# One core, a rotation and three attention blocks: the blocks' prologue inside the setup, scores of two heads as alternating row tiles, and 27 stack transfers

## The chip, the cores and the metric

The kernel runs on one core of one Trainium2 chip. The metric is the device time of one execution in microseconds. The kernel before takes 2118.55 us, the median of three runs.

## The reference

The input `x` has 16 samples of 256 tokens with 288 channels; `cond` has one row of 288 per sample. First, a rotation: a 64-dimensional basis is taken from `P` by a QR factorisation, and each sample gets a rotation of that subspace by the matrix exponential of a skew matrix. Then three attention blocks, alike in form:

```python
v = silu(cond) @ W.T + b                 # 2016 entries of a skew matrix A, per sample
Q, _ = qr(P);  z = x @ Q                 # z @ expm(A) replaces z inside x
x = x + (z @ expm(A) - z) @ Q.T
...
for each of three layers:
    sh_a, sc_a, g_a, sh_m, sc_m, g_m = split(silu(cond) @ W_ada + b_ada, 6)
    h = layer_norm(x) * (1 + sc_a) + sh_a
    q, k, v = heads(h @ W_qkv + b_qkv)   # 16 heads of 18
    x = x + g_a * (softmax(q @ k.T * scale) @ v @ W_proj + b_proj)
    h = layer_norm(x) * (1 + sc_m) + sh_m
    x = x + g_m * (gelu(h @ W_fc1 + b_fc1) @ W_fc2 + b_fc2)   # 288 -> 1152 -> 288
```

## The kernel before

**Two programs one after the other.** `rotation_setup` (L51) does the rotation and the modulation rows of all layers; `layers` (L914) does the blocks. The setup's QR is a Householder sweep in nine phases of up to eight columns on DVE. One column is a chain of small operations: size and sign of the pivot (L771, L772), pivot (L779), turned column (L793), reciprocal (L799), factor (L805), next column (L813), outer product (L819), and the update of the tile (L785); then ACT takes square roots (L374) for `norm_col` (L833). DVE's squarings of the exponential (L724) and PE's pieces (transposes of x L490, its projection L498) fill the gaps. After the QR come the modulation rows (L539, L543), the differences (L625, two samples as two row tiles of 64 rows on PE), the sums on DVE (L906) and 16 stores to the output tensor; SP waits for all of them before `layers` starts. There POOL stages `w_in`, DVE splits it, sample 0 is read back, and its layer norm taken.

**The half-step.** `layers` runs 48 half-steps, one per layer and sample. The work is a software pipeline: in half-step `it` the core does the shifted scores, exponentials and weighted values of sample `it`, the projection and MLP of `it - 1`, and the queries, keys, values and first scores of `it + 1`. Each engine runs its own list of this in an order written by hand; counting semaphores join them.

**Precision.** fp32 data is split in a high and a low part (fp32r). A product is three products, so the three pieces of 18 channels of a head are laid below each other in a stack. `q_stack` and `k_stack` hold eight units of two heads. In `k_stack` each unit has two columns of 256, one for each head, with zeros in the rows of the other head; the two heads of a unit share 108 rows (`PAIR_ROWS`). They are filled from the `qk` tiles by SP in `stacks` (L1199): group A (units 0 to 4) is 9 transfers, 3 of queries (L1189) and 6 of keys (L1195), which wait for the fifth shifted unit of the sample before; group B (units 5 to 7) is 15, and waits for the last shifted unit.

**Scores.** `score_unit` (L1706) is two matmuls of 108 rows and 512 columns into `scores` (L1718), two sets of banks taken in turn. DVE takes the maxima (`unit_max`, L1968) of 128 by 1024 numbers. Unit `u` waits for the maxima of unit `u - 2`, so one unit is always in hand:

```python
if u < 2: pe.wait_ge(s_exp, 8 * it - 1 + u + PRE_EXP)
else:     pe.wait_ge(s_max, 8 * it + u - 1)
```

After all eight, the maxima are transposed (L1728), negated (ACT L1491), and put as one more row each into `q_stack` by two transfers. `shifted_unit` (L1732) then computes scores minus maximum, transposed, in four matmuls of 110 rows and 256 columns (L1741), and ACT takes the exponentials (L1501). The weighted values (L1755, four column tiles of 32) give also the sums; these go by ACT's queue to a scratch tensor and back (L1515, L1520), DVE takes reciprocals (`inverse`, L1973), and four more transfers spread them (L1530) into `inv_sum`. ACT issues the four between the activations of the MLP's hidden tiles, the last after the last of these (L1544). `normalise` (L1980, two DVE operations) waits for them. In DVE's order it stands before the maxima of unit 3; the gating of the MLP's first token tile (`gate_down`, L2016) stands before those of unit 5:

```python
for u in range(8):
    if u == 3:
        normalise(it)
    if u == 5 and before:
        gate_down(it - 1, 0)
    if after:
        unit_max(it + 1, u)
```

PE's list around the scores (L1845 to L1876): `up` (L1780, five uses) makes the hidden tiles, unit 0 comes ahead of the last `up` and unit 1 behind it, then transposes (L1651), then six parts of `down` (L1635 with `w_down`, nine matmuls each, the bias of a tile of tokens L1789), with units 2 to 6 behind the parts 0 to 4 and unit 7 behind unit 6. POOL makes the low parts (L1294), among them those of the hidden tiles.

Of the kernel before, what the change touches and what calls it, by code (L numbers as in the profile page):

```python
# [6 lines left out]
F32 = mybir.dt.float32  # L7
# [8 lines left out]
L = 3  # L16
# [22 lines left out]
PAIR_ROWS, SHIFTED_ROWS = 6 * HD, 6 * HD + 2  # L39
# [11 lines left out]
def rotation_setup(nc, dram, keep):  # L51


# [6 lines left out]
    mods, g_rot, ident = keep["mods"], keep["g_rot"], keep["ident"]  # L60
    with ExitStack() as ctx:
# [3 lines left out]
        def sem(name):  # L65
            return ctx.enter_context(nc.semaphore(name))
# [13 lines left out]
        w_ada = sb("w_ada", [KC + 1, L, NCH, ADA])  # L80

        shared = sb("w_rot_x", [P, R * R * NCH])
        w_rot = [shared[0:KC + 1, n * 1024 * NCH:(n + 1) * 1024 * NCH].rearrange("k (c e) -> k c e", c=NCH) for n in range(4)]
        x_all = shared[:, 0:B * XF].rearrange("p (s t c) -> p s t c", s=B, t=2)
        v_rot = sb("v_rot", [P, 4, SKEW_COLS])
# [7 lines left out]
        ef = sb("ef", [P, NPAIR, 2, R])  # L93
# [19 lines left out]
        size = sb("size", [P, 2])  # L113
# [15 lines left out]
        z_all = sb("z_all", [P, NPAIR, T])  # L129
        f_c = sb("f_c", [P, NPAIR, R])  # L130
# [20 lines left out]
        s_eye = sem("s_eye")  # L151
        s_ready = sem("s_ready")
# [4 lines left out]
        s_v_st = sem("s_v_st")  # L157
        s_a_ld = sem("s_a_ld")
# [20 lines left out]
        s_size = sem("s_size")  # L179
        s_pivot = sem("s_pivot")  # L180
        s_recip = sem("s_recip")
        s_turn = sem("s_turn")
        s_factor = sem("s_factor")
        s_next = sem("s_next")
        s_outer = sem("s_outer")
        s_update = sem("s_update")
# [13 lines left out]
        s_inv_norm = sem("s_inv_norm")  # L200
# [14 lines left out]
        s_out_st = sem("s_out_st")  # L215
# [6 lines left out]
        SQUARES = {5: range(0, 6), 6: range(6, 15), 7: range(15, 24), 8: range(24, FILLS)}  # L222

        PAIRS = {2: (0,), 4: (1, 2), 5: (3,), 6: (4,), 7: (5,), 8: (6,), PHASES: (7,)}
        POWERS_AT, SERIES_AT = 3, 4
# [13 lines left out]

        @block.sync  # L240
        def _(sp):
            sp.dma_start(p_nat[:, :, :], dram["p_nat"]).then_inc(s_p, 16)
            sp.dma_start(unit[GRAM, GRAM_COLS], dram["ident"][0:R, 0:R]).then_inc(s_unit, 16)
            sp.dma_start(unit[TOP, TOP_COLS], dram["ident"][0:R, 0:R]).then_inc(s_unit, 16)
            sp.dma_start(low[GRAM, GRAM_COLS], dram["lower"][:, 1, :]).then_inc(s_low, 16)
# [11 lines left out]
            for n, (a, b) in enumerate(GROUPS):  # L257
                if n == 0:
                    sp.wait_ge(s_skew_ps, 1)
                if n == 1:  # L260
                    sp.wait_ge(s_skew_ps, 4)
                    sp.wait_ge(s_a_ld, 16 * 8)
# [1960 lines left out]
```

## Time and profile before

| | us |
|---|---|
| median of 3 runs (2117.92 to 2121.7) | 2118.55 |
| the profiled execution | 2125.66 |
| its span | 2123.9 |
| PE busy | 1966.4 (93%) |
| DVE / ACT / POOL busy | 1224.8 / 1107.5 / 1015.8 |
| PE matmuls of scores L1718 / L1741, busy | 241.9 / 246.5 |
| maxima L1968, busy | 460.7 |
| starts of the first and of the last maxima transposes (L1728) | 233.56 and 2055.18 |

The span is cut in a setup, from 0 to about 176 us, a filling of the pipeline, and 48 half-steps. Between the first and the last pair of maxima transposes lie 47 intervals; most of the ordinary ones are 37.69 us long, and some with the weights of a new layer are longer. PE's busy time counts the overlap of matmuls once. A row of the timeline gives start, length, engine, line, what is written from what, partitions by elements, and the number of instructions. A matmul's length includes the pipeline; how far starts lie apart tells more of what it costs.

### The profile page before, as it was taken

The numbers are of one execution on the slowest core, as the hardware profiler recorded it, in microseconds if no ns is written. First come the engines' busy times: TensorE is split into PE (matmuls) and PEld (weight loads), VectorE is DVE, ScalarE is ACT, GpSimd is POOL, SyncE is SP. The second block draws the span as 40 slices with busy tenths as digits, with TensorE's granted clock in tenths as the row PEclk, the third lists the DMA queues.
The fourth block names the chain that finished last, engine by engine and source line by source line (L and its number), as shares of the span: only waits on it lengthen the run. The fifth ranks groups of instructions, "written<-read, shape, count | busy, mean of one in ns | idle before, by whom it ended". The sixth has DMA issues, their size and how long they took to land. (4 is left out here: it accounts for less than half of the span.)

```text
span 2123.9 us, 50051 instructions
## 1 busy us (share of the span) xinstructions
PE 1966.4 (93%) x16599; PEld 1746.1 (82%) x16599; DVE 1224.8 (58%) x2813; ACT 1107.5 (52%) x1906; POOL 1015.8 (48%) x1045
## 2 busy tenths in 40 slices
PE   4684599999999999999999999999999999999997
PEld 2553378998989988879989999888789899998986
DVE  7766375565655665574655556575656565565641
ACT  2222346656465564556465564654664655646552
POOL 2002164555545554655545545455645455454544
PEclk9887689999999999999999999999999999999998
DMA  6604243333233333343233333333432333333320
GB/s 167 160 13 142 83 135 107 95 89 99 80 108 91 93 95 95 111 131 100 80 104 88 98 99 84 99 88 93 144 96 81 103 88 99 99 83 100 86 80 25
DMA packets 138669, 207.65 MB, mean 98 GB/s; under 512 B 35204, under 2 KB 95778, under 8 KB 137518
## 3 DMA queue, kind: packets, MB, share of 16 engines
q1 hardware_dynamic: 111742, 171.06, 28.9%
q10 hardware_dynamic: 24192, 27.94, 4.7%
q0 software_dynamic: 2640, 7.44, 1.2%
q8 instruction: 53, 0.87, 0.2%
q14 instruction: 42, 0.34, 0.1%
HBM read 99.81 MB, written 20.82 MB: 57 GB/s over the span
## 5 line engine op out<-in xcount | busy, mean ns | idle before, releaser
L1968 DVE TENSOR_REDUCE maxima<-scores 128x4 f32<-128x1024 f32 x384 | 460.7, 1222 | 185.7 <-PE scores L1718 180.9
L1294 POOL TENSOR_TENSOR hidden<-g_full,hidden 128x512 fp32r<-128x512 f32 (+1 forms) x240 | 280.5, 1177 | 356.8 <-ACT hidden L1544 355.8
L1501 ACT ACTIVATE probs<-scores 128x1024 f32<-128x1024 f32 x384 | 383.2, 1026 | 95.2 <-PE pv_ps L1755 57.1
L1780 PE MATMUL mlp_ps<-h_mlp,w_up 128*128 128x256 f32 (+1 forms) x3024 | 405.6, 287 | 8.2 <-ACT hidden L1544 4.7
L1780 PEld LDWEIGHTS mlp_ps<-h_mlp,w_up 128*128 128x128 f32 (+1 forms) x3024 | 377.5, 191 | 42.0 <-issue 19.3
L1635 PE MATMUL mlp_ps<-w_down,hidden 128*128 128x288 f32 x2592 | 388.1, 294 | 0.0
L1635 PEld LDWEIGHTS mlp_ps<-w_down,hidden 128*128 128x128 f32 x2592 | 368.9, 188 | 18.5
L1718 PE MATMUL scores<-k_stack,q_stack 108*128 108x512 f32 x768 | 241.9, 407 | 22.4 <-DMA k_stack<-qk 18.4
L1741 PE MATMUL scores<-q_stack,k_stack 110*128 110x256 f32 x1536 | 246.5, 293 | 3.3 <-ACT probs L1501 2.0
L1741 PEld LDWEIGHTS scores<-q_stack,k_stack 110*128 110x128 f32 x1536 | 207.8, 191 | 32.1 <-issue 18.9
L1491 ACT ACTIVATE neg_max<-att_ps 16x256 fp32r<-16x256 f32 x48 | 18.0, 375 | 387.7 <-PE att_ps L1728 387.7
L1378 POOL TENSOR_TENSOR o_full<-o_full,inv_sum 128x512 f32<-128x512 f32 x96 | 140.5, 1484 | 156.6 <-DVE o_att L1980 156.6
L1973 DVE RECIPROCAL inv_few<-sums 128x32 f32<-128x32 f32 x48 | 16.9, 353 | 319.9 <-DMA sums<-sum_scratch 319.9
L1543 ACT ACTIVATE g_full<-mlp_ps 128x512 f32<-128x512 f32 (+1 forms) x240 | 133.7, 557 | 129.5 <-PE mlp_ps L1780 61.4
L1294 POOL TENSOR_TENSOR h_mlp<-h_full,h_mlp 128x512 fp32r<-128x512 f32 x48 | 72.6, 1511 | 259.0 <-DVE h_mlp L1934 258.8
L1755 PE MATMUL pv_ps<-probs,v_sb 128*32 128x256 f32 x3072 | 189.4, 388 | 0.6 <-ACT probs L1501 0.6
L1635 PE MATMUL mlp_ps<-w_out,o_att 128*128 128x288 f32 x1152 | 174.2, 302 | 4.0 <-issue 2.9
L1635 PEld LDWEIGHTS mlp_ps<-w_out,o_att 128*128 128x128 f32 x1152 | 159.9, 191 | 6.1 <-issue 3.5
L1718 PEld LDWEIGHTS scores<-k_stack,q_stack 108*128 108x128 f32 x768 | 128.0, 194 | 35.4 <-DMA k_stack<-qk 20.3
L1692 PE MATMUL att_ps<-h_att,w_in 128*126 128x256 f32 (+3 forms) x1008 | 137.6, 284 | 11.8 <-POOL h_att L1294 10.2
L1755 PEld LDWEIGHTS pv_ps<-probs,v_sb 128*32 128x32 f32 x3072 | 91.0, 111 | 65.5 <-issue 4.5
L1692 PEld LDWEIGHTS att_ps<-h_att,w_in 128*126 128x126 f32 (+3 forms) x1008 | 128.1, 185 | 12.9 <-issue 11.7
(221 smaller groups left out, 2865.9 us busy)
## 6 DMA issues: line engine op xcount, KB each, us to landing
q_stack<-qk SPq DMA_DIRECT2D x144, 180.0 KB
k_stack<-qk SPq DMA_DIRECT2D x288, 90.0 KB
inv_sum<-inv_scratch ACTq DMA_DIRECT2D x192, 128.0 KB, 2.7
k_stack<-qk SPq DMA_DIRECT2D x288, 54.0 KB
x_in<-out_x SPq DMA_DIRECT2D x48, 288.0 KB, 3.8
x_mid<-out_x SPq DMA_DIRECT2D x48, 288.0 KB, 4.2
out_x<-x_out SPq DMA_DIRECT2D x48, 288.0 KB, 3.1
q_stack<-qk SPq DMA_DIRECT2D x144, 72.0 KB
```

What stands on the lines that cost most here:

```text
L1294: tt(out, full, high.bitcast(F32), ALU.subtract).then_inc(signal, 1)
L1378: tt(o_full[:, half, :], o_full[:, half, :], inv_sum[:, half, :], ALU.mult).then_inc(s_o_norm, 1)
L1491: evict(neg_max[:, :], att_ps[0:H, 0:T], ACT.Copy, scale=-1.0).then_inc(s_neg, 1)
L1501: evict(probs[:, u % 4, :, :, :], scores[u % 2][:, :, :, :], ACT.Exp, scale=SCALE)\
L1543: evict(g_full[:, n % 2, 0:width], bank[:, 0:width], ACT.Gelu_apprx_tanh).then_inc(s_gelu, 1)
L1635: last = mm(out, a(left), c(weights[w]), start=start and n == 0, stop=stop and n == total - 1)
L1692: last = mm(qk_bank[n][0:cols.stop - cols.start, (m % 2) * T:(m % 2 + 1) * T], w[:, cols], h, start=count == 0, stop=count == 6)
L1718: last = mm(scores[u % 2][:, qt, :, :], q_stack[r, u, qt * P:(qt + 1) * P], k_stack[r, u, :, :], start=True, stop=True)
L1741: last = mm(scores[u % 2][:, par, kt, :], k_stack[r, u, par, kt * P:(kt + 1) * P], q_stack[r, u, :], start=True, stop=True)
L1755: last = mm(pv_ps[32 * i:32 * i + 32, (g % 2) * T:(g % 2 + 1) * T], v_sb[:, kt, 4 * g + i, :], probs[:, u % 4, i % 2, kt, :], start=kt == ...
L1780: last = mm(up_bank[n % 2][:, (m % 2) * T:(m % 2 + 1) * T], w[:, m * P:(m + 1) * P], h, start=count == 0, stop=count == 6)
L1968: nc.vector.tensor_reduce(out=maxima[:, :, :, u], in_=scores[u % 2][:, :, :, :], axis=AX.X, op=ALU.max).then_inc(s_max, 1)
```

## The change

**The prologue in the setup.** `rotation_setup` returns at once. A new function `prepare`, called inside `layers` when only the first tiles are laid out, does the setup. In it POOL also stages the three pieces of `w_in`, ACT makes their high parts in the phases 6 to 8 of the QR and DVE the low parts behind it; ACT fills the constants of `k_stack` and `v_sb`; the rotated sample 0 stays in `x_in`, and its statistics and `x_hat` are made among the sums of the other samples. The wait for the 16 output stores has moved into `layers`. In the QR step the size operation is gone (the pivot is now one operation with the sign), waits are merged, the update stands ahead of the reciprocal and the spreading ahead of `column_norms`. Small loads went to ACT's queue, the `w_rot` loads stand second on SP's, the skew rows go in halves by SP and POOL, powers and series one phase earlier, pair 7 and the modulation rows of layer 0 into the last phase, and only one layer's rows stand among the differences, where two stood.

**Row tiles.** `k_stack` has one set of columns per unit and no zeros. A head's rows start at 0 or at 64, and its 54 rows (55 with the maximum) are multiplied alone, as a row tile. Two heads alternate, and two units are done in one visit, which waits for both units before:

```diff
-            def score_unit(it, u):
+            def score_units(it, u):
 
                 if u == 0:
                     pe.wait_ge(s_stack_a, PIECES_A * (it + 1) + 16)
-                if u == 5:
+                    pe.wait_ge(s_exp, 8 * it + PRE_EXP)
+                else:
+                    pe.wait_ge(s_max, 8 * it + u)
+                if u == 4:
                     pe.wait_ge(s_stack_b, PIECES_B * (it + 1) + 16)
-                if u < 2:
-                    pe.wait_ge(s_exp, 8 * it - 1 + u + PRE_EXP)
-                else:
-                    pe.wait_ge(s_max, 8 * it + u - 1)
-                r = slice(0, PAIR_ROWS)
-                for qt in range(2):
-                    last = mm(scores[u % 2][:, qt, :, :], q_stack[r, u, qt * P:(qt + 1) * P],
-                              k_stack[r, u, :, :], start=True, stop=True)
-                last.then_inc(s_score, 1)
+                    pe.wait_ge(s_stack_k, PIECES_K * (it + 1))
+                for v in (u, u + 1):
+                    for qt in range(2):
+                        for par in range(2):
+                            r = slice(R * par, R * par + HEAD_ROWS)
+                            last = mm(scores[v % 2][:, par, qt, :], q_stack[r, v, qt * P:(qt + 1) * P],
+                                      k_stack[r, v, :], start=True, stop=True, tile_position=(R * par, 0))
+                    last.then_inc(s_score, 1)
...
+            def shifted_units(it, u):
 
                 if u == 0:
                     pe.wait_ge(s_neg_st, 32 * it + 32 + 16)
-                if u >= 2:
-                    pe.wait_ge(s_exp, 8 * it + u - 1 + PRE_EXP)
+                else:
+                    pe.wait_ge(s_exp, 8 * it + u + PRE_EXP)
...
                 for n in range(6):
+                    if after and n % 2 == 0:
+                        score_units(it + 1, n + 2)
                     if before:
                         down(m, n // 3, n % 3)
-                    if after and n < 5:
-                        score_unit(it + 1, n + 2)
-                    if after and n == 4:
-                        score_unit(it + 1, 7)
```

`score_units(it + 1, 0)` stands ahead of the fourth `up` (n of 3). ACT's list now has the exponentials of units 0 and 1 between the first and the second query and key eviction. DVE's list in the half-step is as it was.

**The transfers.** Each of 27 moves 18 rows. Group A is 12 by SP, group B 9 queries by SP, and the 6 keys of units 5 to 7 go by POOL, in `last_keys`, behind the same condition as group B:

```diff
                 for j in range(3):
-                    into_stack(j, Q_PARTS[j], slice(0, 5), slice(0, PAIR), slice(0, 5), s_stack_a)
-                for j in range(3):
                     for par in range(2):
-                        head_into_stack(j, par, K_PARTS[j], slice(0, 5), PAIR + HD * par, slice(0, 5), s_stack_a)
+                        head_into_stack(sp, q_stack, j, par, Q_PARTS[j], slice(0, 5), HD * par, slice(0, 5), s_stack_a)
+                        head_into_stack(sp, k_stack, j, par, K_PARTS[j], slice(0, 5), PAIR + HD * par, slice(0, 5), s_stack_a)
...
+            def last_keys(it, first=False):
...
+                if not first:
+                    pool.wait_ge(s_st, 8 * it + PRE)
...
+                        head_into_stack(pool, k_stack, j, par, K_PARTS[j], slice(2, 5), 2 * PAIR + HD * par, slice(5, 8), s_stack_k)
```

**How the instructions move.** First PE's list, from the third to the seventh unit of scores (`scores<-k_stack,q_stack`) among the parts of `down` (`mlp_ps<-w_down,hidden`). Before:

```order
L1718 MATMUL scores<-k_stack,q_stack 128x512 x2
L1635 MATMUL mlp_ps<-w_down,hidden 128x288 x9
L1718 MATMUL scores<-k_stack,q_stack 128x512 x2
L1791 REGISTER_ALU
L1635 MATMUL mlp_ps<-w_down,hidden 128x288 x9
L1715 REGISTER_ALU
L1718 MATMUL scores<-k_stack,q_stack 128x512 x2
L1789 MATMUL mlp_ps<-b_down,ones_l 128x288
L1635 MATMUL mlp_ps<-w_down,hidden 128x288 x9
```

The same place of the change, the third and fourth unit, the fifth and sixth:

```order
L1824 MATMUL scores<-k_stack,q_stack 128x256 x8
L1895 ISA
L1896 MATMUL mlp_ps<-b_down,ones_l 128x288
L1898 REGISTER_ALU
L1739 MATMUL mlp_ps<-w_down,hidden 128x288 x18
L1816 REGISTER_ALU
L1818 ISA
L1819 REGISTER_ALU
L1824 MATMUL scores<-k_stack,q_stack 128x256 x8
```

Where one unit stood behind nine matmuls, two now stand ahead of eighteen.

SP's list, the transfers of one sample into the stacks, before:

```order
L1189 DMA q_stack<-qk 36x1280 x3
L1195 DMA k_stack<-qk 18x5x256 x6
L1189 DMA q_stack<-qk 36x512
L1195 DMA q_stack<-qk 18x256 x2
L1189 DMA q_stack<-qk 36x512
L1195 DMA q_stack<-qk 18x256 x2
L1189 DMA q_stack<-qk 36x512
L1195 DMA q_stack<-qk 18x256 x2
L1195 DMA k_stack<-qk 18x3x256 x6
```

The end of group A and the beginning of group B in the change (ten transfers like the first two stand ahead):

```order
L1282 DMA q_stack<-qk 18x1280
L1282 DMA k_stack<-qk 18x1280
L1282 DMA q_stack<-qk 18x768
L1282 DMA q_stack<-qk 18x512
L1282 DMA q_stack<-qk 18x256
```

Group A has grown from 9 to 12 transfers, group B on SP shrunk from 15 to 9.

## Rows read from the trace of the kernel before

**Rows 1.** One half-step: busy time (instructions) of each engine, granted clock, DMA share, GB/s.
```profile
1000.00:1037.70 37.70, 37.70 (x320) 34.40 (x319) 21.53 (x40) 21.83 (x36) 19.75 (x20) 1.00 0.35 94
```

**Rows 2.** The page's costliest groups: busy time, mean ns, idle before and releaser.
```profile
L1718 PE MATMUL scores<-k_stack,q_stack 108*128 108x512 f32 x768 | 241.9, 407 | 22.4 <-DMA k_stack<-qk 18.4
```

**Rows 3.** PE's timeline in that half-step, first scores and `down`.
```profile
1045.08 0.38 PE L1789 MATMUL mlp_ps<-b_down,ones_l 128*128 128x288 f32 x1
...
1046.49 0.63 PE L1718 MATMUL scores<-k_stack,q_stack 108*128 108x512 f32 x2
1046.95 1.36 PE L1635 MATMUL mlp_ps<-w_down,hidden 128*128 128x288 f32 x9
1048.15 0.63 PE L1718 MATMUL scores<-k_stack,q_stack 108*128 108x512 f32 x2
```

**Rows 4.** PE's timeline in the setup, row tiles of 64 rows, two samples.
```profile
168.09 0.51 PE L625 MATMUL chain_a<-g_rot,z_all 64*128 64x288 f32 x1
...
168.10 0.51 PE L625 MATMUL ps_a<-g_rot,z_all 64*128 64x288 f32 x1
...
168.43 0.40 PE L625 MATMUL chain_a<-g_rot,z_all 64*128 64x288 f32 x1
...
168.68 0.40 PE L625 MATMUL chain_b<-g_rot,z_all 64*128 64x288 f32 x1
```

**Rows 5.** PE's timeline, weighted values and the `up` behind them.
```profile
1034.69 1.94 PE L1755 MATMUL pv_ps<-probs,v_sb 128*32 128x256 f32 x32
1036.56 1.88 PE L1780 MATMUL mlp_ps<-h_mlp,w_up 128*128 128x256 f32 x14
```

**Rows 6.** PE's timeline at two narrow stretches: starts two groups of four apart.
```profile
1035.58 0.61 PE L1755 MATMUL pv_ps<-probs,v_sb 128*32 128x256 f32 x8
...
1036.02 0.61 PE L1755 MATMUL pv_ps<-probs,v_sb 128*32 128x256 f32 x8
```

**Rows 7.** DVE's timeline around the maxima of one half-step.
```profile
1047.15 1.23 DVE L1968 TENSOR_REDUCE maxima<-scores 128x4 f32<-128x1024 f32 x1 [1.22 <-PE scores L1718]
1048.29 1.28 DVE L1980 TENSOR_TENSOR o_att<-o_full,inv_sum 128x512 fp32r<-128x512 f32 x2
1049.49 2.35 DVE L1968 TENSOR_REDUCE maxima<-scores 128x4 f32<-128x1024 f32 x2
1051.76 0.45 DVE L2016 TENSOR_TENSOR gated<-mlp_ps,gate_f 128x288 f32<-128x288 f32 x1
```

**Rows 8.** Issues on SP's queue (SPq, group A) and on ACT's (ACTq).
```profile
1028.81 2.58 SPq L1189 DMA_DIRECT2D q_stack<-qk  x3
1031.43 5.85 SPq L1195 DMA_DIRECT2D k_stack<-qk  x6
...
1044.59 0.59 ACTq L1530 DMA_DIRECT2D inv_sum<-inv_scratch  x1
```

**Rows 9.** Part 6 of the page: issues, KB each, us from issue to landing.
```profile
inv_sum<-inv_scratch ACTq DMA_DIRECT2D x192, 128.0 KB, 2.7
```

**Rows 10.** POOL's timeline in the filling of the pipeline: issues of transfers.
```profile
177.72 1.69 POOL L1303 DMA_DIRECT2D staging<-in_w_in  x3 [0.83 <-POOL minus_half L1277]
```

**Rows 11.** Waits before 180 us: who waited for whom, total, times, longest.
```profile
DVE norm_col L833 <- ACT gram_norm L374: 11.0, 5, 5.2
```

**Rows 12.** PE's timeline from the end of the QR to the first queries and keys.
```profile
136.48 0.86 PE L490 MATMUL xt_ps<-ident,w_rot_x 128*96 128x128 f32 x6
...
141.05 1.37 PE L539 MATMUL ada_ps<-w_ada,silu_c 96*16 96x352 f32 x8
...
153.66 0.79 PE L539 MATMUL ada_ps<-w_ada,silu_c 96*16 96x352 f32 x8
...
156.30 0.70 PE L438 MATMUL xt_ps<-u_t,f_c 64*64 64x288 f32 x4
...
187.66 1.09 PE L1651 MATMUL att_ps<-ident,x_hat 128*128 128x128 f32 x4 [14.73 <-DVE x_hat L1921]
...
199.32 3.25 PE L1692 MATMUL att_ps<-h_att,w_in 128*126 128x256 f32 x14 [10.15 <-POOL h_att L1294]
```

More of the change, by code:

```diff
@@ new lines, in layers @@
+        b_down = sb("b_down", [P, C], F32R)
+        ones = sb("ones_l", [P, P], F32R)
+        warm = sb("warm", [P, 1])
+        x_mid = sb("x_mid", [P, 2, C])
+        x_one = sb("x_one", [P, 2, C])
+        x_out = sb("x_out", [P, 2, C])
+        gated = sb("gated", [P, 2, C])
+        gate_a = sb("gate_a", [P, C])
+        gate_f = sb("gate_f", [P, C])
+        h_full = sb("h_full", [P, 3, T])
+        h_att = [sb(f"h_att{i}", [P, 3 - i, T], F32R) for i in range(2)]
+        h_mlp = [sb(f"h_mlp{i}", [P, 3 - i, T], F32R) for i in range(2)]
@@ new lines, in layers @@
+        qk = [sb(f"qk{i}", [QK_ROWS, QK_TILES, T], F32R) for i in range(2)]
+        q_stack = sb("q_stack", [P, H // 2, T], F32R)
+        maxima = sb("maxima", [P, 2, 2, H // 2])
+        neg_max = sb("neg_max", [H, T], F32R)
+        probs = sb("probs", [P, 4, 2, 2, T])
+        o_full = sb("o_full", [P, 2, 512])
+        sums = sb("sums", [P, 32])
+        inv_few = sb("inv_few", [P, 32])
+        inv_sum = sb("inv_sum", [P, 2, 512])
+        o_att = [sb(f"o_att{i}", [P, 2, 512], F32R) for i in range(2)]
@@ new lines, in in_place @@
+        def in_place(name, shape):
+            with nc.sbuf_tensor(f"{name}_raw", shape, F32) as raw:
+                pass
+            return raw, sb(f"{name}1", shape, F32R)
+        w_up = [sb("w_up0", [P, 3, FF], F32R)]
+        up_raw, up_low = in_place("w_up", [P, 2, FF])
+        w_up.append(up_low)
+        w_down = [sb("w_down0", [P, NF, C], F32R)]
+        down_raw, down_low = in_place("w_down", [P, NF, C])
+        w_down.append(down_low)
+        hidden = [sb(f"hidden{i}", [P, NF, T], F32R) for i in range(2)]
@@ L1165, in at, with head_into_stack @@
             return isinstance(b, int) and b == n
+        Q_PARTS, K_PARTS = (0, 1, 0), (0, 0, 1)
+        def head_into_stack(engine, stack, j, par, part, src, row, units, signal):
+            first = R * par + HD * j
+            engine.dma_start(stack[first:first + HD, units, :].bitcast(F32),
+                             qk[part][row:row + HD, src, :].bitcast(F32)).then_inc(signal, 16)
         @block.sync
```

609 lines of the change are left out of this document (313 added, 296 removed).

## The prediction

> **What bounds the kernel now.** I read the view of stretches first, then PE's timeline of one half-step, then the waits, and last DVE's timeline and the queues around the two places where PE's list changes. In a half-step PE has no gap at the full granted clock, while DVE, ACT and POOL are busy for 21.53, 21.83 and 19.75 of 37.70 us [rows 1]. So 48 half-steps are bound by PE, and what another engine gains is worth nothing there unless PE waits for it. Ahead of them it is otherwise: PE stood still for 14.73 and 10.15 us before it had its first queries and keys at 199.32 [rows 12], and the score matmuls waited 18.4 us for keys in their stack, all in the first samples [rows 2]. The change touches both parts. It shortens the first, once. In the second it alters PE's work and the order of the waits, 46 to 47 times, so that 0.1 us per half-step weighs as much as 4.7 us of setup.
>
> **PE's work per half-step.** A unit of scores costs 0.46 us before (from 1046.49 to the next start at 1046.95) [rows 3], a shifted unit about the same, so two units 0.94. In the change two units are eight matmuls of 256 columns, in four pairs. The nearest rows for two row tiles are those of the setup: the two start 0.01 apart, so they run at once, and pairs follow each other by 0.25, only after the first by 0.34 [rows 4]. Those are fp32; the split data streams 512 columns in 0.23 [rows 3], so a pair of 256 columns costs 0.12 and four 0.48. What is left is the price of the change between whole rows and tiles. Leaving tiles is seen behind the weighted values: eight groups take 8 x 0.22 = 1.74 [rows 6], but the next `up` starts 1.87 after the first [rows 5], 0.13 more, and entering shows 0.34 - 0.25 = 0.09 [rows 4]. The matmul behind the first also looked late in narrower stretches, so I take 0.2 for a change, 0.4 for a visit. Then a visit costs 0.88, against 0.94: a gain of 0.06, in eight visits 0.5 us per half-step. The ends: 0.48 for a visit if a change of tiles costs nothing, 1.36 if two row tiles did not run at once.
>
> The Trainium skill speaks of both. "TensorE: Matmul & The Clock Gate", "Measured speedup vs the span model", gives the span of packed matmuls as the duration of one plus about 4 ns for each further tile, with no term for a change; by that a visit would cost about 0.5. "TensorEngine Tiling (Array Packing)", "Key Properties", says that a change of the tiling mode drains TensorE, without a price. The rows with 0.13 and 0.09 more [rows 4 to 6] side with the second.
>
> **The waits that pairs bring.** Before, a unit waited for the unit two ahead of it; one unit was always in hand while DVE read the other. Now both banks must be read before a visit begins, and DVE's list is unchanged, so what stands in it between two maxima comes on the path.
>
> *Units 4 and 5* wait for the maxima of unit 3, ahead of which the normalisation stands. From the start of the visit for 2 and 3: 0.66 until the first maxima start (1046.49 to 1047.15) [rows 3, 7], 1.14 for them, 1.20 for the normalisation (1048.29 to 1049.49), 1.22 for the second and 0.05 for the signal: 4.27. PE meanwhile has the visit, 0.88, and two parts of `down` with the bias, 1.41 + 1.20 = 2.6 [rows 3]: 3.5. It stands for 0.8. More, if the sums' reciprocals come late: the last of the four transfers that spread them is issued behind the last hidden tile at 1044.59 [rows 8] and lands 2.7 later [rows 9], at 1047.3, 1.0 ahead of its reader now. In the change this tile is finished about 0.4 later, since a whole visit stands ahead of the fourth `up`, while the visit for 2 and 3 comes ahead of `down` and so 1.4 earlier. The normalisation then starts some 0.8 late and the stand is 1.6. I take 1.4.
>
> *Units 6 and 7* wait for the maxima of unit 5, ahead of which stands the gating of the first token tile, which needs the third part of `down`. From the visit for 4 and 5: 0.88 + 1.20 for the part, some 0.3 until DVE reads it, 0.45 for the gating, 1.22 for the maxima: 4.05, against 0.88 + 1.20 + 1.41 = 3.5 on PE. 0.55.
>
> *Group A.* Nine transfers are issued in 8.5 us (1028.81 to 1037.28) [rows 8], keys 0.98 and queries 0.86 each. The new ones are contiguous on both sides, as the queries were, and half as tall; I take 0.82, an estimate, and twelve give 9.8. The ends: 0.75, or 0.98 as the keys now, 9.0 and 11.8. Their release, the fifth shifted unit, comes with the sixth now, behind the first weighted values; they land some 2 us behind the last issue. Their reader, the visit for 0 and 1, has moved 1.7 us ahead, from the fifth `up` to the fourth. By this account it waits 0.2 to 0.5; I take 0.35, and 1.7 for the upper end.
>
> *Shifted units.* ACT needs 1.0 per unit and has PE's other work beside it; only pairs wait for pairs. 0.2.
>
> The sum: -0.5 + 1.4 + 0.55 + 0.35 + 0.2 = **+2.0**; part of a stand is slack for the next (a late visit for 0 and 1 makes the normalisation less late), so I take **+1.9**. In 46 half-steps: +87.
>
> *POOL's six* cost 6 x 0.56 = 3.4 us of POOL [rows 10]. They stand between the low part of the MLP's input and the first hidden tile, where POOL has nothing to do; it is busy for 19.75 of 37.70 [rows 1]. Nothing, if they land before the visit for 4 and 5, some 8 us later. Without this cover the hidden tiles, and `down` with them, would come up to 3.4 late.
>
> **The setup, once.** The QR: the waits for ACT's roots, 11.0 in five phases [rows 11], shrink since the spreading and ACT's roots no longer stand in front of each other, and PE's first loads come earlier: -8, between 0 and -15. One operation of a step less of nine, but the pivot is a longer one on the chain behind the sign: 0, between -7 and +5. Pair 7 out of the stretch behind the QR: 136.48 to 141.05, -4.6 [rows 12]. One layer's modulation rows fewer in the differences: 153.66 to 156.30 [rows 12], -3 with the columns. From there to the first queries and keys at 199.32: PE's stand for the normalised sample 0 is gone but for some 4 us, -10.9; POOL's low part need not wait for staging, -5.1; the wait for the last stores, -2. Together **-34**. First group A +1.2, the first scores with a shorter group B -3.4, and the stack waits of the first two half-steps, 7 of the 18.4 [rows 2], -7. All once: **-43**, between -25 and -58.
>
> **The sum.** The profiled execution took 2125.66 (span 2123.9). 2125.7 - 43 + 87 = 2169.7. The median of the runs is 7.1 below the profiled one, so it becomes **2162**.
>
> **Rivals.** *(a) Changing tiles costs next to nothing*: a visit 0.5 to 0.55, -3.2 per half-step. The stands grow, since DVE's chain does not shrink: 1.75 for units 4 and 5, 0.6, 0.65 for group A, 0.6 for the shifted pairs: +3.6. That is +0.4, 19 in all, and with the setup 2095: faster. For it: rows 4 show only 0.09 for entering. Against it: 0.13 for leaving, and the unchanged list of DVE. It decides from +0.8 per half-step downwards, where the setup's gain still pays. Cheaper waits at the price I forecast (the slack absorbs most) end in the same place; both together 0.22. (The skill's span rule is this case.) *(b) Row tiles are serial here*: a visit 1.36, +3.8 after shorter stands, 2118 - 43 + 175 = 2250. Against it stand the two starts 0.01 apart [rows 4], though of fp32 and 288 columns; 0.06. *(c) Transfers are late*: group A at 0.98 each and POOL's six not landed before units 4 and 5: another +1.1, 2212; 0.12. *(d) The setup gains little*, -15, with the loss as forecast: 2190; 0.06. *(e) The merged waits cost nothing and changes do, so nothing moves*: 0.04.
>
> **How the numbers follow.** My forecast, 2162 with 2130 to 2190 around it, has 0.5. What the measurement can tell from no change is 0.2%, 4.2 us. Faster by more: (a), 0.24 with the fringe of (e). Within: 0.05. Slower: the rest, 0.71. The range takes in (a)'s point, 2095, with 7 below it, and (c) up to 2212; outside stay (b) and the far side of (a). 2088 to 2212.
>
> **What would show it.** Right: intervals of the maxima transposes near 39.6; gaps on PE of about 1.4 and 0.6 us before the visits for 4 and 6, released by DVE's maxima, and DVE idle before the normalisation for a spread transfer; the two heads' matmuls 0.01 apart with a visit of 0.9; first queries and keys near 165. Wrong: visits of 0.5 to 0.6, or maxima that are always ahead (the loss is then too large); or gaps before the visit for 0 released by a stack transfer of over 1 us; or a granted clock below 1.00 in the half-steps, which I count as none because the gaps are short.

## The result and the profile after

The changed kernel takes 2316.37 us (median of 4 runs, 2307.9 to 2326.05), the kernel before 2119.69 beside it. The ratio is 1.093 (95% interval 1.088 to 1.098): slower by 197 us. The forecast was 2162, slower by 43. The direction was right and the size was not, and the range (to 2212) does not hold it.

The profiled execution has a span of 2312.1 us against 2123.9, 188.2 more. The starts of the maxima transposes cut it in three. The first pair comes at 209.53 instead of 233.56 (the setup gained 24.0); from there to the last pair, at 2237.18, lie 2027.6 us instead of 1821.6 (206.0 more in 47 intervals, 4.4 each); the rest is 74.9 instead of 68.7 (6.2 more).

Part 1 of the page of the changed kernel; it answers to the row of before in the table ahead, PE 1966.4 (93%):

```profile
PE 1980.1 (86%) x17367; PEld 1690.4 (73%) x17367; DVE 1210.3 (52%) x2735; ACT 1111.2 (48%) x1930; POOL 1156.3 (50%) x1319
```

PE is busy for more time and a smaller share. Two half-steps of the changed kernel that follow each other, in the view of stretches (columns as in [rows 1]):

```profile
1037.50:1078.40 40.90, 36.92 (x336) 31.95 (x335) 21.57 (x40) 21.78 (x36) 22.86 (x26) 1.00 0.31 87
1078.40:1121.40 43.00, 39.96 (x337) 35.03 (x335) 21.57 (x40) 21.77 (x36) 22.85 (x26) 0.92 0.30 82
```

The first runs at the full clock. PE's work has fallen from 37.70 to 36.92, and 4.0 us of standing have come. The second is 2.1 us longer: PE's busy time has 3.0 more for the same matmuls, its standing 0.9 less, and the granted clock is 0.92. So there are two losses, gaps and a slower clock.

PE's timeline of the changed kernel in one half-step, first scores (L1824) and `down`:

```profile
1017.99 0.74 PE L1824 MATMUL scores<-k_stack,q_stack 54*128 54x256 f32 x8 [1.60 <-DMA k_stack<-qk]
1018.67 2.77 PE L1887 MATMUL mlp_ps<-h_mlp,w_up 128*128 128x256 f32 x21
...
1022.02 0.73 PE L1824 MATMUL scores<-k_stack,q_stack 54*128 54x256 f32 x8
1022.69 0.40 PE L1896 MATMUL mlp_ps<-b_down,ones_l 128*128 128x288 f32 x1
1022.93 2.54 PE L1739 MATMUL mlp_ps<-w_down,hidden 128*128 128x288 f32 x18
1028.83 0.74 PE L1824 MATMUL scores<-k_stack,q_stack 54*128 54x256 f32 x8 [3.36 <-DVE maxima L2072]
1029.50 1.45 PE L1739 MATMUL mlp_ps<-w_down,hidden 128*128 128x288 f32 x9
1030.79 0.29 PE L1896 MATMUL mlp_ps<-b_down,ones_l 128*128 128x288 f32 x1
...
1032.70 0.50 PE L1824 MATMUL scores<-k_stack,q_stack 54*128 54x256 f32 x4 [0.43 <-DVE maxima L2072]
```

A visit of two units takes 0.67 (1028.83 to 1029.50), and the nine matmuls behind it 1.29 where they took 1.20 [rows 3]: 0.76 in all, not 0.88. Row tiles and their changes are cheaper than forecast. Three of the four visits wait: 1.60 for the keys' stack, 3.36 for DVE, 0.43 for DVE. DVE at the same time:

```profile
1018.51 0.35 DVE L2077 RECIPROCAL inv_few<-sums 128x32 f32<-128x32 f32 x1 [8.49 <-DMA sums<-sum_scratch]
...
1022.57 1.23 DVE L2072 TENSOR_REDUCE maxima<-scores 128x4 f32<-128x1024 f32 x1 [1.50 <-PE scores L1824]
1026.17 1.29 DVE L2084 TENSOR_TENSOR o_att<-o_full,inv_sum 128x512 fp32r<-128x512 f32 x2 [2.37 <-DMA inv_sum<-inv_scratch]
1027.38 1.22 DVE L2072 TENSOR_REDUCE maxima<-scores 128x4 f32<-128x1024 f32 x1
```

DVE itself stands 2.37 us ahead of the normalisation, for the transfers that spread the reciprocals. These are late from their start. ACT's queue issues the store of the sums (`sum_scratch`), and the load behind it as soon as the store has landed. Before:

```profile
1037.33 0.53 ACTq L1515 DMA_DIRECT2D sum_scratch<-o_full  x1
1039.36 0.35 ACTq L1520 DMA_DIRECT2D sums<-sum_scratch  x1
```

and in the change:

```profile
1012.52 0.54 ACTq L1619 DMA_DIRECT2D sum_scratch<-o_full  x1
1016.21 0.36 ACTq L1624 DMA_DIRECT2D sums<-sum_scratch  x1
```

From issue to issue 2.03 us before, 3.69 now, for the same 16 KB. The load's issue stands ahead of the second hidden tile in ACT's list, so ACT stands too. The waits from 300 to 2000 us, changed kernel (total, times, longest):

```profile
PE scores L1824 <- DVE maxima L2072: 101.5, 67, 6.3
...
ACT g_full L1647 <- DMA sum_scratch<-o_full: 63.2, 23, 4.6
PE scores L1824 <- DMA k_stack<-qk: 57.9, 37, 2.5
```

101.5 + 57.9 = 159.4 us of PE's standing in some 40 half-steps, 4.0 each: 1.5 ahead of units 0 and 1, 2.3 ahead of 4 and 5, 0.3 ahead of 6 and 7. In the old kernel the score matmuls waited 0.6 us in that stretch. The clock fits: in the second of the two half-steps in the view of stretches two stretches of 5 us read

```profile
1095.00:1100.00 5.00, 4.65 (x39) 4.35 (x35) 0.00 (x0) 1.99 (x4) 1.51 (x2) 1.00 0.56 154
1100.00:1105.00 5.00, 3.88 (x25) 3.75 (x26) 2.56 (x3) 2.68 (x6) 2.56 (x2) 0.74 0.25 60
```

with a gap of 1.47 us that ended at 1101.12; behind it 21 `up` matmuls took 4.28 us where they take 2.77 at 1018.67. The clock was at its lower level (1.2 GHz) for a part of it. In the first of the two, gaps of 1.3 and 2.2 us left it at 1.00, so a lower clock follows a gap at times and not always. Over the whole trace the granted clock is below 1.00 in 32 of the 47 intervals of the change, and in 7 of those of the kernel before.

### The profile page after: what moved, and what is told of

It reads as the page before. It is cut to its first block and busy times, and to the rows that moved or that the text cites. A ratio compares the mean times of both kernels' runs of the same rounds, so it can differ in the third digit from the quotient of the medians.

```text
span 2312.1 us, 51564 instructions
## 1 busy us (share of the span) xinstructions
PE 1980.1 (86%) x17367; PEld 1690.4 (73%) x17367; DVE 1210.3 (52%) x2735; ACT 1111.2 (48%) x1930; POOL 1156.3 (50%) x1319
## 5 line engine op out<-in xcount | busy, mean ns | idle before, releaser
L1887 PE MATMUL mlp_ps<-h_mlp,w_up 128*128 128x256 f32 (+1 forms) x3024 | 437.0, 300 | 4.7 <-POOL h_mlp L1395 3.5
L1887 PEld LDWEIGHTS mlp_ps<-h_mlp,w_up 128*128 128x128 f32 (+1 forms) x3024 | 397.2, 202 | 40.5 <-issue 20.5
L1739 PE MATMUL mlp_ps<-w_down,hidden 128*128 128x288 f32 x2592 | 410.9, 313 | 0.0
L1824 PE MATMUL scores<-k_stack,q_stack 54*128 54x256 f32 x1536 | 150.8, 317 | 218.0 <-DVE maxima L2072 135.2
L1824 PEld LDWEIGHTS scores<-k_stack,q_stack 54*128 54x128 f32 x1536 | 109.9, 197 | 259.3 <-issue 196.7
L1862 PE MATMUL pv_ps<-probs,v_sb 128*32 128x256 f32 x3072 | 200.5, 391 | 0.8 <-ACT probs L1605 0.8
L1282 POOL DMA_DIRECT2D k_stack<-qk x288 | 152.7, 538 | 31.4 <-PE scores L1848 21.9
L1848 PE MATMUL scores<-q_stack,k_stack 55*128 55x256 f32 x1536 | 146.1, 310 | 4.4 <-ACT probs L1605 3.1
L1796 PE MATMUL att_ps<-h_att,w_in 128*108 128x256 f32 (+3 forms) x1008 | 137.5, 284 | 6.0 <-POOL h_att L1395 5.3
L1848 PEld LDWEIGHTS scores<-q_stack,k_stack 55*128 55x128 f32 x1536 | 106.4, 190 | 49.2 <-ACT probs L1605 29.7
L1862 PEld LDWEIGHTS pv_ps<-probs,v_sb 128*32 128x32 f32 x3072 | 86.0, 111 | 66.8 <-issue 12.9
```

Of the source, the lines that this page charges most:

```text
L1282: engine.dma_start(stack[first:first + HD, units, :].bitcast(F32), qk[part][row:row + HD, src, :].bitcast(F32)).then_inc(signal, 16)
L1739: last = mm(out, a(left), c(weights[w]), start=start and n == 0, stop=stop and n == total - 1)
L1796: last = mm(qk_bank[n][0:cols.stop - cols.start, (m % 2) * T:(m % 2 + 1) * T], w[:, cols], h, start=count == 0, stop=count == 6)
L1824: last = mm(scores[v % 2][:, par, qt, :], q_stack[r, v, qt * P:(qt + 1) * P], k_stack[r, v, :], start=True, stop=True, tile_position=(R * ...
L1848: last = mm(scores[v % 2][:, par, kt, :], k_stack[r, v, kt * P:(kt + 1) * P], q_stack[r, v, :], start=True, stop=True, tile_position=(R * ...
L1862: last = mm(pv_ps[32 * i:32 * i + 32, (g % 2) * T:(g % 2 + 1) * T], v_sb[:, kt, 4 * g + i, :], probs[:, u % 4, i % 2, kt, :], start=kt == ...
```

## The experiments

Fifteen versions were run; "load at" is the time from the issue of the sums' store to that of their load, "interval" the distance of the maxima transposes, both medians over half-steps of the profiled execution. Times are medians of all executions; the profiled one was 9 us or more above its median in three versions (2212 for the normalisation with a late load, 2137 for the four edits, 2174 for POOL in two parts), so their intervals read a little long.

| version | us | interval | load at |
|---|---|---|---|
| before | 2119.7 to 2123.3 | 37.70 | 2.04 |
| the change | 2316.4 | 42.33 | 3.96 |
| scores one unit at a time | 2240.7 | 41.32 | 3.99 |
| normalisation before unit 4 | 2189.7 | 39.20 | 3.96 |
| first visit later | 2299.2 | 41.47 | 4.05 |
| before, with pairs | 2280.0 | 41.10 | 2.04 |
| six keys on SP | 2291.0 | 42.03 | 2.37 |
| normalisation, late load | 2187.3 | 40.53 | 4.01 |
| the same, group A split | 2174.2 | 39.10 | 3.77 |
| single, late load | 2201.5 | 39.77 | 4.00 |
| four edits (POOL later) | 2128.1 | 37.90 | 2.39 |
| the same, all on SP | 2267.2 | 41.60 | 2.38 |
| single units, all on SP | 2123.3 | 38.27 | 2.38 |
| before, POOL's six | 2286.2 | 41.67 | 4.79 |
| POOL later alone | 2291.9 | 41.83 | 2.40 |
| POOL in two parts | 2160.5 | 38.82 | 2.39 |
| three and three | 2179.9 | 40.44 | 2.41 |

**Scores one unit at a time**, at the old places and with the old waits:

```diff
-                else:
-                    pe.wait_ge(s_max, 8 * it + u)
...
+                if u < 2:
+                    pe.wait_ge(s_exp, 8 * it - 1 + u + PRE_EXP)
+                else:
+                    pe.wait_ge(s_max, 8 * it + u - 1)
...
-                for v in (u, u + 1):
+                for v in (u,):
```

> The change, but the unit scores are made one unit at a time, at the places and with the waits of the kernel before (a unit waits for the unit two ahead); row tiles, transfers, setup and the pairs of shifted units stay. Theory W (the merged waits of the pairs of units make the loss, and the slower clock follows from PE's gaps): a unit costs 0.45, as before, the gaps before the third and fourth visit (2.4 and 0.3 us per half-step) go, the clock comes back to 1.00 in the ordinary half-steps, the interval of the maxima transposes falls from 42.3 to about 37.5 and the time to 2080 to 2100. Theory T (late transfers make it: 12 in group A and POOL's six): the wait for the keys' stack before unit 0 and the late sums stay, interval 40 to 41, time 2220 to 2260.

2240.7 lies in the range of theory T, and the load of the sums is at 3.99, as it says; the wait for keys ahead of unit 0 did not stay, since unit 0 comes one `up` later. The waits of PE for DVE's maxima went, as theory W said (101.5 us to under 4), but another of 71.7 us took their place.

```profile
ACT g_full L1647 <- DMA sum_scratch<-o_full: 72.8, 27, 3.3
PE mlp_ps L1888 <- ACT hidden L1648: 71.7, 39, 2.5
```

The store of the sums lands late, ACT stands for it, its second hidden tile is late, and so is PE's fourth `up`. So the merged waits are one cause and late transfers another, and in the change the stands ahead of the visits covered part of the second.

**The normalisation ahead of unit 4:**

```diff
-                    if u == 3:
+                    if u == 4:
                         normalise(it)
```

> The change with one line of DVE's list moved: the normalisation stands ahead of the maxima of unit 4 instead of unit 3. Theory W: the visit for units 4 and 5 no longer waits for the normalisation, nor for the transfers that spread the reciprocals; its gap of 2.4 us per half-step goes, that of the visit for 6 and 7 grows from 0.3 to about 1.3; the interval falls by 1.5 to 2.5, clock included, and the time by 70 to 120, to 2200 to 2245. If the clock is a cause of its own, or the transfers set the end, it falls by less than 30.

2189.7, 127 below the change, a little more than expected for one moved line: the largest part of the loss that a single edit gives back. The gap ahead of units 4 and 5 went; ahead of 6 and 7 it is 0.6 per half-step, and ahead of 0 and 1 still 1.6.

**The first visit one `up` later:**

```diff
-                        if after and n == 3:
+                        if after and n == UP_USES - 1:
                             score_units(it + 1, 0)
```

> The change with the visit for units 0 and 1 one use of up later, ahead of the last one, where unit 0 stood before. It now waits 1.5 us for the keys' stack. Theory T: that wait goes and the interval falls by 1 to 1.5 us, the time by 50 to 80. Theory W: PE then stands in the fourth up instead, since ACT's second hidden tile is late (it stands behind the wait for the sums' store), or the later maxima lengthen the gap before units 4 and 5; the time falls by less than 30 or rises.

2299.2, 17 less. The wait for keys went from the visit, and PE stood in the fourth `up` instead, 71.4 us for ACT's hidden tile from 300 to 2000: theory W's case, with the late store as its cause.

**The kernel before with pairs of units**, stacks, matmuls and transfers as they were:

> The kernel before with one part of the change: scores two units at a visit, with its merged waits and its places in PE's list. Stacks, transfers, matmuls of 108 rows and setup stay. Theory W: the visits for 4 and 6 wait for DVE as in the change; gaps of 0.8 to 2 and 0.3 to 0.6 us per half-step, interval 39 to 40.5, time 2180 to 2250. Theory T: with the old transfers nothing is late, interval below 38.2 and time below 2145.

2280.0, above the range that was expected. Its waits from 300 to 2000 us:

```profile
PE scores L1718 <- DVE maxima L1964: 63.4, 56, 3.0
...
PE scores L1718 <- DMA k_stack<-qk: 49.3, 22, 3.1
```

With the old transfers too, and that I had not thought of: the visit for 4 and 5 needs group B, one unit earlier than the unit 5 alone did, and SP's 15 issues come too late for it. Merged visits at the places of the change cost 157 us on the old kernel by themselves (2123.3 beside it).

**The six keys issued by SP**, behind its nine, and none by POOL:

> The change, but the six transfers of keys of units 5 to 7 are issued by SP behind its nine, and POOL issues none. In the change the store of the sums lands 1.9 us later than before (the load behind it is issued 3.96 instead of 2.04 after the store). Theory P (POOL's six crowd the DMA engines at that time): the load is issued at 2.0 to 2.7 again, the reciprocals' spread lands 1.5 us earlier, the interval falls by 1 to 1.5 us, the time to 2240 to 2275. Theory A (the twelve of group A do it, on SP's queue): the load stays at 3.5 to 4, the time within 20 of the change's 2316, or more if the last six land too late for units 4 and 5.

The load of the sums at 2.37: theory P, though the time is above its range. The gap ahead of the first visit went as well, and so POOL's six had delayed group A, not its own twelve issues. But SP issues the six behind its other 21, some 8 us after the load of the sums; so this run moves them in time as well as to another queue. But the six now come too late for units 4 and 5, and the sum is a gain of 25 only:

```profile
PE scores L1823 <- DMA k_stack<-qk: 97.1, 33, 3.3
```

**Normalisation and a late load of the sums** in ACT's list:

```diff
-                load_sums(it)
                 if before:
                     gelu(it - 1, 1)
+                load_sums(it)
```

> The change with the normalisation ahead of the maxima of unit 4, and in ACT's list the load of the sums behind the second hidden tile instead of ahead of it, so that ACT does not stand for the store with the tile behind it. Against the version with the first of these edits (2190): if the late second tile adds to the gap before the visit for 0 and 1, the time falls by 20 to 60; if only the keys' stack makes this gap (1.6 per half-step, released by a transfer of keys), it is 2180 to 2200.

2187.3 against 2189.7: the second case. Ahead of the first visit only the keys count.

**Group A split** between SP and POOL, keys of units 5 to 7 behind SP's nine, on top of the version before it:

> The version before it, and POOL issues the six transfers of keys of group A instead of those of units 5 to 7, which go behind SP's nine of group B. Group A is then issued in about half the time. Theory T2 (12 issues of 0.74 in a row make units 0 and 1 late): the gap of 1.6 us goes, the interval falls from about 38.8 to 36.5 to 37.5, and the time to 2060 to 2130, below the kernel before. If it is the landing under load rather than the issue, the gap stays above 1.0 and the time above 2140.

2174.2: the gap ahead of the first visit went (0.1 per half-step), as the first case has it, and the time stayed above 2140, as the second has it. The load is at 3.77: POOL's transfers of group A delay the sums as those of units 5 to 7 did. The waits for DVE grew (ahead of units 6 and 7 to 1.0, of 2 and 3 to 0.35), and PE stands 0.5 ahead of `down` for ACT's last hidden tile.

**Single units and a late load:**

> Scores one unit at a time at the old places, as in the first experiment (2241, with one gap of 1.7 us per half-step in the fourth up, released by ACT's hidden tile), and ACT's load of the sums behind the second hidden tile. If ACT standing for the store of the sums makes that gap: it goes, the interval is 37.0 to 38.0 and the time 2070 to 2120. If the tile is late for another reason: above 2200.

2201.5, inside the band that was to speak against it by a hair. The wait in the fourth `up` did go; 54.2 us in front of `down` for ACT's last hidden tile came in its place. Moving ACT's wait moved the stand.

**Four edits** (normalisation ahead of 4, gating ahead of 6, POOL's six behind its first hidden tile, small loads on SP first):

```diff
                     for n in range(UP_USES):
                         hidden_low(it - 1, n)
+                        if n == 0 and after:
+                            last_keys(it + 1)
```

> The change with four edits: the normalisation ahead of the maxima of unit 4, the gating of the first token tile ahead of those of unit 6, POOL's six transfers behind its first hidden tile instead of ahead of it, and the four small loads of the QR's start on SP's queue ahead of the w_rot loads. If POOL's six are what delays the store of the sums and group A: the load of the sums is issued 2.0 to 2.6 after the store (3.96 in the change), the gap before the visit for 0 and 1 falls from 1.6 to below 0.5, that for 6 and 7 to below 0.3; interval 36.5 to 38, time 2060 to 2120. The QR starts its first step at about 7.5 instead of 11.95 and the first maxima transposes come 4 to 5 earlier, 201 to 205. If it is group A on SP's queue: the gap of 1.6 stays, time above 2150.

2128.1 (ratio to before 1.003, interval 1.0015 to 1.005): 188 of the 197 us are back, though the time is 8 us above the expected range. Load at 2.39, the clock at 1.00 in 37 of 47 intervals (40 in the kernel before). What is left:

```profile
1029.78 3.12 POOL L1282 DMA_DIRECT2D k_stack<-qk  x6
1032.92 4.51 POOL L1395 TENSOR_TENSOR hidden<-g_full,hidden 128x512 fp32r<-128x512 f32 x4
...
1034.30 0.60 ACT L1649 ACTIVATE g_full<-mlp_ps 128x512 f32<-128x512 f32 x1 [2.42 <-POOL hidden L1395]
...
1036.25 0.40 PE L1898 MATMUL mlp_ps<-b_down,ones_l 128*128 128x288 f32 x1 [1.00 <-ACT hidden L1650]
```

POOL's six issues take 3.12 us, its next low part waits behind them, ACT's fourth tile for that, and PE 1.00.

**The same with all transfers on SP:**

> As the one before, but with the six issued by SP behind its nine (as in the experiment that gave 2291), POOL issues none. The load of the sums at 2.4, no gap before units 0 and 1. What is left is whether the last key lands before the visit for 4 and 5: 27 issues of 0.74 are 20 us behind the release. If it does, the interval is 36.5 to 38 and the time 2050 to 2120; if not, a gap of 1 to 3 us before that visit released by a transfer of keys, and 2140 to 2200.

2267.2, above what its bad case allowed: PE waits for keys, 112.8 us from 300 to 2000. For pairs the 27 issues of one queue, 0.74 us each, are a bound of their own.

**Single units, all on SP**, the old waits, no POOL:

> Scores one unit at a time at the old places with the old waits, shifted units in pairs, all 27 transfers on SP's queue, DVE's and ACT's lists as in the change, small loads on SP first. Theory: nothing is left that stands before PE but the pairs of shifted units, and those gain 0.27 per visit pair. Interval 36.5 to 37.5, clock 1.00 but for the special half-steps, time 2040 to 2095, faster than the kernel before. If even then the sums are late or the second hidden tile is: above 2120.

2123.3, the same as before (1.0007, 0.9994 to 1.0019), not faster. No waits of weight are left (0.8 per half-step in all, 0.6 before). What eats the gain is the change of tiles, which a single unit pays as often as a pair:

```profile
1034.40 0.50 PE L1824 MATMUL scores<-k_stack,q_stack 54*128 54x256 f32 x4
1034.83 1.46 PE L1738 MATMUL mlp_ps<-w_down,hidden 128*128 128x288 f32 x9
1036.22 0.50 PE L1824 MATMUL scores<-k_stack,q_stack 54*128 54x256 f32 x4
```

0.43 for the unit and 1.39 for the nine behind it, 1.82 where it was 0.46 + 1.20 = 1.66 [rows 3]. Eight times 0.16 are 1.3 us; the pairs of shifted units give back 4 x (0.94 - 0.76) = 0.7; the interval is 0.6 longer.

**The kernel before with POOL's six alone:**

> The kernel before with one part of the change: the six transfers of keys of units 5 to 7 are issued by POOL, at the place of the change; all else as it was. If POOL's six crowd out the others whatever the layout: the load of the sums is issued 3 to 4 instead of 2.04 after the store, ACT's second hidden tile and with it the fourth up come late, a gap of 0.5 to 2 per half-step, time 2145 to 2220. If it needs the twelve of group A beside them: within 10 of 2120.

2286.2, 165 more than before, for six transfers of 54 KB moved to another queue, and with that to another time: SP issued them from 7 us behind the store of the sums, POOL from 3.5 us ahead of it. It is well above the expectation, and the clearest run of the study:

```profile
1017.05 0.53 ACTq L1534 DMA_DIRECT2D sum_scratch<-o_full  x1
...
1021.19 0.35 ACTq L1539 DMA_DIRECT2D sums<-sum_scratch  x1
1021.72 0.60 ACT L1562 ACTIVATE g_full<-mlp_ps 128x512 f32<-128x512 f32 x1 [2.79 <-DMA sum_scratch<-o_full]
```

```profile
1022.85 2.74 PE L1800 MATMUL mlp_ps<-h_mlp,w_up 128*128 128x256 f32 x14 [1.97 <-ACT hidden L1563]
```

```profile
1013.54 3.73 POOL L1412 DMA_DIRECT2D k_stack<-qk  x6 [0.60 <-issue]
```

POOL issues from 1013.54 to 1017.3; the store issued at 1017.05 lands by 1021.2, in 4.1 us instead of 2.0; ACT stands 2.79, PE 1.97, and the fourteen matmuls behind that gap take 2.55 us to the next start where fourteen took 1.72 before the gap (from 1016.28), at a lower clock. ACT's stand for the store is 133.5 us from 300 to 2000, PE's for ACT's hidden tile 99.6.

**POOL's six later, nothing else:**

> The change with one edit: POOL's six transfers stand behind its first hidden tile instead of ahead of it; normalisation, gating and small loads as in the change. Theory P (their place crowds out group A and the sums): the load of the sums is issued 2.4 after the store, the gap before units 0 and 1 (1.5 per half-step) goes, that before units 4 and 5 shrinks but stays, since the normalisation still stands ahead of unit 3's maxima: interval 39 to 41, time 2170 to 2260. If the two causes were one and the same, the time would be near the 2128 of the version with all four edits.

2291.9, 24 less. Load at 2.40 and first visit in time (0.1 per half-step), as theory P has it, but above the range. The wait for DVE ahead of units 4 and 5 did not shrink, 2.4 per half-step for 2.3, and a new gap of 1.1 stands ahead of `down`, since POOL's low parts now wait behind its six issues:

```profile
PE scores L1826 <- DVE maxima L2074: 110.3, 65, 6.8
...
PE mlp_ps L1898 <- ACT hidden L1650: 43.9, 39, 2.6
```

The normalisation is hardly earlier. The load of the sums gained 1.6 us, but the last part of the spread lands 12.1 us after the store of the sums instead of 12.9: the six stand beside the store of the reciprocals now, which lands 2.6 us after its issue instead of 1.6. The edits add up to more than their parts: 127 for the normalisation alone, 24 for POOL alone, 188 for all four. How much of the rest the gating and the small loads give was not measured by itself.

**POOL's six in two parts**, three behind the first and three behind the third hidden tile:

> The version with four edits (2128), and POOL's six in two parts, three behind its first and three behind its third hidden tile. There the six in a row kept POOL for 3.1 us, ACT's fourth hidden tile waited 2.4 for POOL's low part, and PE stood 1.0 per half-step ahead of down. In threes: this gap falls below 0.3 and the time to 2075 to 2105, faster than the kernel before by 15 to 45. If another wait takes its place (the last three keys landing behind the visit for 4 and 5, or POOL's fourth low part late for down): 2110 to 2150.

2160.5, worse by 32. The gap ahead of `down` did fall (1.0 to 0.3 per half-step), but its second three stand beside the spread of the reciprocals: from the issue of its last part to its landing it takes 4.3 us instead of 2.7, and units 4 to 7 wait.

**Three by POOL, three by SP:**

> The version with four edits (2128), but POOL issues only the three transfers of the keys of the even heads of units 5 to 7 behind its first hidden tile, and SP the other three among its nine, 24 in all. If POOL being held by six issues makes the last gap (1.0 per half-step ahead of down), three issues halve it and nothing falls on the reciprocals' spread: gap below 0.3, time 2075 to 2110. If SP's 24 issues of 0.74 bring the last keys too late (17.8 us behind the release, 2 to 3 to land) a gap of 0.5 to 1 before units 4 and 5 takes its place: 2110 to 2140.

2179.9, above its bad case. PE's timeline:

```profile
1047.10 0.40 PE L1898 MATMUL mlp_ps<-b_down,ones_l 128*128 128x288 f32 x1 [0.48 <-ACT hidden L1650]
...
1051.52 0.73 PE L1826 MATMUL scores<-k_stack,q_stack 54*128 54x256 f32 x8 [1.68 <-DMA k_stack<-qk]
```

POOL's half halves the one gap (0.48), and SP's 24 issues make another (1.68).

## Why the prediction was wrong

**What bounds the kernel: right.** PE in the half-steps, and waits that come from elsewhere weigh 47 times.

**"A visit costs 0.88, against 0.94": too dear.** 0.76. The streaming term (0.48) was right, pairs start 0.11 apart; the change of tiles was 0.28 for both, not 0.4. If all eight visits cost this, they give back 1.4 per half-step by their starts; by PE's busy time it is 0.8, and why the two differ is not shown. The forecast was 0.5. The ends (0.48 and 1.36) held it. The Trainium skill has two pages on this, "TensorE: Matmul & The Clock Gate", "Measured speedup vs the span model", and "TensorEngine Tiling (Array Packing)", "Key Properties". The trace agrees with the second in kind: there is a price at each change, 0.28 a visit, and it shows also in the matmuls behind. It agrees with the first that tiles run at once (the two heads' matmuls start 0.01 apart), and not with a span that has no term for a change.

**"Units 4 and 5 ... I take 1.4": the place and mechanism were right, the size was not.** 2.3 per half-step by the trace, since the last of the spread lands 12.9 us after the store of the sums instead of 10.1. I counted only that it is issued 0.4 later. Here the step failed: the durations of the store and of the spread were taken from a trace in which SP's transfers stood beside them and POOL issued none. Not all of the 2.8 us is POOL's: with all 27 transfers on SP the last part still lands at 11.7 to 11.8, and takes 3.8 to 3.9 us from its issue instead of 2.8.

**"Group A ... I take 0.35": 1.5.** An issue cost even less than I took (0.74 against 0.82). What delayed the group was POOL's six; without them at that place the gap is 0.15 (six keys on SP) and 0.1 (POOL later).

**"POOL's six ... Nothing, if they land before": the step that failed behind the two before it.** I asked what POOL's time costs and whether the six land in time, and not whom they delay. Alone on the old kernel they cost 165 us, and the merged visits alone 157. In the change the two overlap: the normalisation's place alone gives back 127, POOL's place alone 24, both with the two smaller edits 188.

**"A granted clock below 1.00 ..., which I count as none because the gaps are short": wrong.** Of the two half-steps shown, the one with the lower clock is 2.1 us longer. The 15 intervals of the change at the full clock take 40.8 to 42.3 us, median 41.2; the 32 others have a median of 43.0, with gaps no longer than theirs (3.9 us an interval against 4.3). By 1.8 us for each of the 32 the clock's part is some 60 us in all, an estimate, or 1.3 a half-step. In the four-edit version, with one gap of 1.0 in an ordinary half-step, this part is gone. That the gaps lower the clock is inferred from this; no run changes the clock alone.

**Units 6 and 7: 0.3, for 0.55. Shifted units: nothing, for 0.2.** So against +1.9 per half-step the median interval shows +4.6: -0.8 for PE's work, 2.3, 1.5 and 0.3 for the stands, and 1.3 for the clock.

**The setup: -24 to the first maxima, for -36.** The stretch behind the QR gave what was forecast: from `c_mat` to the first queries 63.9 us before (135.46 to 199.32) and 37.9 after (137.96 to 175.89), 26 less, as the sum of its terms (-4.6 -3 -10.9 -5.1 -2). The QR failed: forecast -8, found +2.5. Two waits of DVE before 180 us:

```profile
DVE spread L722 <- DMA unit<-in_ident: 7.7, 1, 7.7
...
DVE spread L901 <- PE chain_a L502: 7.1, 5, 5.0
```

The small loads of its start moved to ACT's queue and stood beside the large `w_rot` loads: DVE waited 7.7 us, where it waited 2.05. With them on SP's queue ahead of the large ones (four edits) the wait is 2.79. The same mistake again, a small transfer beside large ones. The other wait accounts for most of the rest: that for ACT's roots did go, 11.0 to 0.2 us, but the spreading, which now stands ahead, waits 7.1 us for PE where it waited 0.3. The stretch varies from execution to execution: `c_mat` starts at 133.2 to 138.2 in the nine traces with the setup of the change, at 132.5 to 135.4 in the five with the small loads ahead, and at 133.5 to 135.5 in the three with the old setup. So the QR gained nothing that shows, and the small loads' place some 3 us.

**The rivals.** (c), transfers late, was the one that happened, and I gave it 0.12 and a price of 1.1. It had group A late and the six themselves late, not the sums. (a) was half right in its price of a visit, and right in that the stands grow as the visit shrinks; its 1.75 for units 4 and 5 was too little too, and its sum had neither POOL's six nor the clock.

**Left open.** That POOL's transfers delay the small transfers beside them is shown at every place tried; why is not. Nor is it shown that the queue makes the difference: wherever SP issued the six, they also came at another time, and a run with POOL's six at SP's time was not made. Which part of the 188 us each of the four edits gives is not separated. A steady state of the old kernel behind the new setup was not tried, since the new setup fills a stack of half the size. No version here beats the kernel before.

## What to carry to other kernels

A transfer moved to an idle queue is not free because the engine is idle. Look at what small, latency-bound transfers are in flight at that time, and follow who waits for their landing. Merging two waits in one takes away the unit in hand, and everything that stands between the two in the other engine's list comes on the path; move that first, and check what each merged visit now needs earlier. Where a kernel is bound by PE at its full clock, price a gap with the slower matmuls behind it, not by its own length.

## What the hardware showed that I had not expected

A 16 KB store took 2.04 us to be followed by its load, and 4.8 when POOL had issued six transfers of 54 KB ahead of it; with SP issuing six such transfers some 8 us after that load, 2.37. A gap of 1.5 to 2 us of PE is at times followed by matmuls at the lower clock (21 in 4.28 us instead of 2.77) and at times not; in the half-step of the timeline above even 3.36 us left the clock at 1.00. The price of leaving row tiles shows also behind them: the nine matmuls that follow take 1.29 to 1.39 us instead of 1.20.
